# Attention units ordered by block of queries, with plain fp32 P V in column tiles and the projection and norm moved inside them

## The reference, cut to what matters

```
ln   = layernorm(layernorm(x)) * g_l + b_l;  xn = layernorm(ctx) * g_x + b_x
q    = ln @ Wq.T;  k, v = concat(xn @ Wkv.T, ln @ Wlkv.T)      # 4 heads of 64
P    = softmax(rmsnorm(q) * gq * 64**-0.5 @ (rmsnorm(k) * gk).T, context keys masked)
x2   = x + (P @ v) @ Wo.T + bo
x3   = layernorm(x2);  two best of 8 experts by softmax(x3 @ router.T)
out  = x2 + sum over the two of  weight * ((silu(gate) * up) @ w2)   # gate, up = x3 @ w13
```

## Time and profile before

| | us |
|---|---|
| median of 3 runs | 1198.23 |
| lowest and highest | 1196.29, 1199.64 |
| span of the profiled execution, first to last instruction | 1197.7 |
| PE, DVE busy in it | 1054.0 (88%), 774.5 (65%) |
| ACT, POOL busy in it | 656.9 (55%), 518.0 (43%) |

### The profile page before, as it was taken

One profiled execution on the slowest core, in us unless ns is written; L12 is line 12 of the kernel. 1 busy time (PEld: TensorE's weight loads), 2 busy tenths in 40 slices (PEclk: granted clock), 3 DMA queues, 4 the chain that ended last, 5 costly groups with the idle time before them and its releaser, 6 DMA issues.

```text
span 1197.7 us, 19749 instructions
## 1 busy us (share of the span) xinstructions
PE 1054.0 (88%) x4904; PEld 761.3 (64%) x4905; DVE 774.5 (65%) x1474; ACT 656.9 (55%) x867; POOL 518.0 (43%) x525
## 2 busy tenths in 40 slices
PE   3688689999999999999999999999866268999994
PEld 2455457667666666766666766666555257888884
DVE  4999777766766866766766676686554813444442
ACT  1455446777777777777677677777522012333321
POOL 4012125454544654644645554465410014555553
PEclk9899879999999999999999999999977569999998
DMA  5222402112131111231211211111266777333332
GB/s 162 62 71 71 172 16 69 53 40 70 53 113 58 60 46 53 66 114 45 71 48 48 70 53 49 57 58 47 67 184 209 265 248 199 52 49 52 53 53 26
DMA packets 84392, 100.41 MB, mean 84 GB/s; under 512 B 11035, under 2 KB 78044, under 8 KB 83836
## 3 DMA queue, kind: packets, MB, share of 16 engines
q1 hardware_dynamic: 73694, 89.20, 22.8%
q0 software_dynamic: 7488, 10.23, 5.3%
q10 hardware_dynamic: 3166, 0.46, 0.3%
HBM read 57.60 MB, written 42.26 MB: 83 GB/s over the span
## 4 chain that ended last, share of the span: by engine, by line
PE 70%; DVE 10%; ACT 7%; DMA 5%; issue 5%; SPq 1%; ACTq 1%; DVEq 0%; POOL 0%; POOLq 0%
PE bM L1177 9%; PE bPV L1241 8%; PE bPV L1239 8%; PE bPV L1249 8%; PE bS L1221 7%; PE bS L1222 7%; ACT PT L642 4%; DVE mpart L867 3%; DMA xin<-x 3%; PE bA L1129 2%; PE bG L1340 2%; PE bH L1357 1%; ACT Ph L648 1%; PE bY L1340 1%; PE bY L1342 1%
## 5 line engine op out<-in xcount | busy, mean ns | idle before, releaser
L482 POOL TENSOR_TENSOR Pl<-PT,Ph 128x1024 fp32r<-128x1024 f32 x96 | 230.8, 2404 | 348.5 <-ACT Ph L648 348.5
L867 DVE TENSOR_REDUCE mpart<-bM 128x1 f32<-128x464 f32 x524 | 310.9, 635 | 87.2 <-PE bM L1177 85.9
L642 ACT ACTIVATE PT<-bS 128x1024 f32<-128x1024 f32 (+1 forms) x240 | 239.4, 998 | 139.3 <-PE bS L1222 139.3
L648 ACT CAST Ph<-PT 128x1024 fp32r<-128x1024 f32 (+1 forms) x240 | 245.5, 1023 | 7.0
L894 DVE TENSOR_TENSOR Pl<-PT,Ph 128x1024 fp32r<-128x1024 f32 x144 | 176.1, 1223 | 104.6 <-ACT Ph L648 104.4
L1221 PE MATMUL bS<-Q,S 128*128 128x512 f32 x464 | 185.9, 401 | 1.4 <-ACT Q L633 0.7
L1239 PE MATMUL bPV<-Ph,V 128*65 128x512 f32 x464 | 184.5, 398 | 0.0
L1222 PE MATMUL bS<-Q,S 128*128 128x512 f32 x464 | 184.0, 396 | 0.0
L1241 PE MATMUL bPV<-Ph,V 128*64 128x512 f32 x464 | 183.1, 395 | 0.0
L1177 PE MATMUL bM<-S,Q 128*128 128x464 f32 (+1 forms) x524 | 165.5, 390 | 10.9 <-DVE mpart L867 8.7
L1249 PE MATMUL bPV<-Pl,V 128*65 128x512 f32 x464 | 146.9, 395 | 0.8
(11 more groups left out here) (210 smaller groups left out, 1537.4 us busy)
## 6 DMA issues: line engine op xcount, KB each, us to landing
W<-wsp_d SPq DMA_DIRECT2D x32, 768.0 KB, 5.8
wraw<-w SPq DMA_DIRECT2D x96, 128.0 KB, 2.2
wsp_d<-whi SPq DMA_DIRECT2D x96, 128.0 KB, 1.7
wsp_d<-wraw SPq DMA_DIRECT2D x96, 128.0 KB, 1.7
v_d<-Vs SPq DMA_DIRECT2D x29, 258.0 KB, 3.3
V<-v_d SPq DMA_DIRECT2D x4, 1870.5 KB, 7.6
xall<-x SPq DMA_DIRECT2D x1, 2048.0 KB, 13.6
xin<-x SPq DMA_DIRECT2D x16, 128.0 KB, 3.8
```

The source lines that it names most:

```text
L482: pool.tensor_tensor(Pl[:, p % 3, :, :], PT[:, p % 3, :, :], Ph[:, p % 3, :, :].bitcast(F32), ALU.subtract)\
L642: act.activation(PT[:, p % 3, 0:w, :], bS[sl][:, 0:w, :], ACT.Exp).then_inc(sem("exp"), 1)
L648: act.copy(Ph[:, p % 3, 0:w, :], PT[:, p % 3, 0:w, :]).then_inc(sem("p_hi"), 1)
L867: dve.tensor_reduce(mpart[:, i, g:g + 1], banks[k % len(banks)][:, 0:PIECE], AX, ALU.max)\
```

## The change

- Units go by block of queries, then by head: four units in a row make all heads of 512 rows. The loops are written out.
- Queries are kept transposed and scaled in `QT` (two more PE transposes and one ACT copy a row tile in the prologue), so `q_T` and its staging go. The outputs of the heads take their place in `QT`.
- V stays in SBUF, unsplit. P V is plain fp32: for each pair of key tiles two matmuls with 64 columns of weights, which write partitions 0 to 63 and 64 to 127 of bPV. The exponential is used as it is; `Ph` and `Pl` go, and there are four buffers of PT.
- The softmax sums come from adding the PT tiles: 11 additions of 128x1024 a unit on POOL, two on DVE, two merging ones on POOL. `o_T` now has eight plain fp32 matmuls in place of four transposes.
- Projection, residual, norm and logits of 12 row tiles are done in units 4 to 15, one tile a unit; four tiles are left for after the last unit.
- The weight split leaves the attention: experts 4 to 7 are split on POOL in the prologue, in 24 chunks of 512 columns, and DVE waits for all of them before it clears Q2. Experts 0 to 3 are loaded whole when the last exponential is done and are split by ACT and POOL in 12 chunks of 1024 during the routing.

The diff, cut to its core:

```diff
+QW = QB * P
+NPT = 4
+EARLY = 4
-WC = 256
+WC = 512
+SC = 1024
+def run_units(body):
+    for b in range(NB):
+        for h in range(H):
+            body(Unit(b, h))
 # SP
+            for n in range(NSPL):
+                sp.wait_ge(sem("wsplit"), n + 1)
+                sp.dma_start(wsp_d[e, 0, :, c:c + WC], whi[:, n % 2, :].bitcast(F32)).then_inc(sem(f"wst{n % 2}"), 16)
+                sp.dma_start(wsp_d[e, 1, :, c:c + WC], wraw[:, n % 2, :]).then_inc(sem(f"wst{n % 2}"), 16)
+                sp.wait_ge(sem(f"wst{n % 2}"), 32 * (n // 2) + 32)
+                if n + 2 < NSPL:
+                    load(n + 2)
...
+            sp.wait_ge(sem("pv"), NP * UNITS)
+            for i in range(QB):
+                sp.dma_start(x2t[:, i, :], xt[NF + i, :, :]).then_inc(sem(f"xin_t{i}"), 16)
 # POOL
+            run_steps(pool, 0, NC + 2, k_mask)
+            for n in range((E - EARLY) * NCH):
+                pool.tensor_copy(whi[:, n % 2, :], wraw[:, n % 2, :]).then_inc(sem("whi"), 1)
+                pool.tensor_tensor(wraw[:, n % 2, :].bitcast(F32R), wraw[:, n % 2, :],
+                                   whi[:, n % 2, :].bitcast(F32), ALU.subtract).then_inc(sem("wsplit"), 1)
+            def z_sum(w, n):
+                pool.wait_ge(sem("exp"), NP * w.u + max(p, q) + 1)
+                pool.tensor_tensor(acc_p[:], one, PT[:, q % NPT, :, :], ALU.add).then_inc(sem("z_p"), 1)
...
+            for n in range(EARLY * NSC):
+                pool.wait_ge(sem("w_hi"), n + 1)
+                pool.tensor_tensor(W[:, e, 1, c:c + SC], W[:, e, 1, c:c + SC].bitcast(F32),
+                                   W[:, e, 0, c:c + SC].bitcast(F32), ALU.subtract).then_inc(sem("w_in"), 1)
 # ACT
+            def unit(w):
+                    act.activation(PT[:, p % NPT, 0:n, :], bS[(w.h + p) % 2][:, 0:n, :], ACT.Exp).then_inc(sem("exp"), 1)
+                    if p == HEADS_AT and w.h % 2 == 0 and not w.first:
+                        heads_T(w)
+                    if p == SD_AT and w.fin:
+                        sd(w.tile, sd2[:], mv2[:])
+                    if p == X3T_AT and w.fin:
+                        act.copy(x3T[:], bT[:, 0, DIM:2 * DIM].rearrange("p (k c) -> p k c", k=2)).then_inc(sem("x3T"), 1)
+            for e in range(EARLY):
+                act.dma_start(W[:, e, 1, 0:N13]..., w13[e, :, :]...).then_inc(sem(f"raw_e{e}"), 16)
+                act.dma_start(W[:, e, 1, N13:EW]..., w2[e, :, :]...).then_inc(sem(f"raw_e{e}"), 16)
+            o_copy(UNITS)
...
+                act.copy(W[:, e, 0, c:c + SC], W[:, e, 1, c:c + SC].bitcast(F32)).then_inc(sem("w_hi"), 1)
 # DVE
-                    dve.tensor_tensor(Vs[:, t.par, :, D + 1:VW], heads(bV[t.par][:, 0, 0:DIM]),
-                                      Vs[:, t.par, :, 0:D].bitcast(F32), ALU.subtract).then_inc(sem("v_lo"), 1)
+            dve.wait_ge(sem("wsplit"), (E - EARLY) * NCH)
 # PE
-                    for b, c in tiles:
-                        pe.matmul(bPV[0:D + 1, 0, :], V[:, h % 2, c, 0:D + 1], Ph[:, sl, b, :], ...)
-                        pe.matmul(bPV[0:D, 0, :], V[:, h % 2, c, D + 1:VW], Ph[:, sl, b, :], ...)
-                        pe.matmul(bPV[0:D + 1, 0, :], V[:, h % 2, c, 0:D + 1], Pl[:, sl, b, :], ...)
+                    for b, c in enumerate(range(2 * p, min(2 * p + 2, NK))):
+                        last = pe.matmul(bPV[b * D:(b + 1) * D, 0, :], V[:, c, h * D:(h + 1) * D],
+                                         PT[:, p % NPT, b, :], start=c < 2, stop=c >= NK - 2, skip_group_check=True)
+            def o_T(n):
+                for i in range(QB):
+                    pe.matmul(bT[:, 0, at:at + D], oT_a[:, i * P:(i + 1) * P], twin[:], start=True, stop=True)
+                    last = pe.matmul(bT[:, 0, at + D:at + D + 1], acc_d[:, 0, i * P:(i + 1) * P], onec[:], ...)
+                for p in range(NP):
+                    scores(p)
+                    if p == OUT_AT and not w.first:
+                        o_T(u)
+                    if p == HEADS_AT and h % 2 == 0 and not w.first:
+                        heads_T()
+                    if p == Y_AT and w.fin:
+                        project(t, bT[:, 0, 0:DIM])
+                    if p == X3T_AT and w.fin:
+                        x3_T(t, bT[:, 0, DIM:2 * DIM], x3[:])
+                    if p == LG_AT and w.fin:
+                        route(t, bT[:, 0, 0:E], x3T)
+                    pieces(p, 0)
+                    if p >= LAG:
+                        outputs(p - LAG)
+                    pieces(p, 1)
+PIECES = ((0, 1), (2, 0)) + ((2, 1),) * 3 + ((1, 1), (2, 1), (1, 1), (2, 1)) + ((1, 1),) * 5 + ((0, 0),)
+OUT_AT, HEADS_AT, Y_AT, SD_AT, X3T_AT, LG_AT = 5, 7, 8, 9, 11, 12
+LAG = 2
+POOL_SUMS = ((0, 1),) + tuple((-1, p) for p in range(2, 12))
+DVE_SUMS = ((12, 13), (-1, 14))
```

More of the change, by code:

```diff
@@ L312, in load @@
[L312 to L323, removed]
-                sp.wait_ge(sem("wsplit"), NCH * i + ch + 1)
-                for part, buf in enumerate((whi[:, ch % 2, :].bitcast(F32), wraw[:, ch % 2, :])):
-                    half, c = divmod(ch, NCH // 2)
-                    sp.dma_start(wsp_d[4 * e + 2 * part + half, :, c * WC:(c + 1) * WC], buf).then_inc(sem(f"wst{ch % 2}"), 16)
-                sp.wait_ge(sem(f"wst{ch % 2}"), 32 * (NCH // 2 * i + ch // 2) + 64)
@@ L332, in expert_split @@
[L332 to L336, removed]
-            EH = E // H
-            for h in range(H):
-                if h < H - 1:
-                    with sp.Fori(0, EH) as i:
-                        expert_split(EH * h + i, False)
-                else:
-                    for e in range(EH * h, E):
-                        expert_split(e, e == E - 1)
-                if h + 2 < H:
-                    sp.wait_ge(sem("pv"), 3 + NP * NB * (h + 1))
-                    v_load(h + 2)
@@ new lines, in pt_free, with sd @@
+            def pt_free(w, p):
+                old = p - NPT if p >= NPT else max(q for q in range(NP) if q % NPT == p)
+                n = w.u if p >= NPT else w.u - 1
+                act.wait_ge(sem("pv"), NP * n + old + 1)
+                for name, sums in (("z_p", POOL_SUMS), ("z_d", DVE_SUMS)):
+                    for m, pair in enumerate(sums):
+                        if old in pair:
+                            act.wait_ge(sem(name), len(sums) * n + m + 1)
+            def sd(t, to, mv):
+                act.wait_ge(sem("mv2"), t + 1)
+                after(act, sem("rs2"), t)
+                act.activation(to, mv[:, 1:2], ACT.Sqrt, bias=eps[:, 0:1]).then_inc(sem("sd2"), 1)
@@ new lines, in unit @@
+            def unit(w):
+                u, v, t = w.u, w.u + 1, w.tile
+                k = 0
+                for p in range(NP):
+                    if p == OUT_AT and not w.first:
+                        o_out(u, (w.h - 1) % H, w.pairs)
+                    if p == Y_AT and w.fin:
+                        stats2(t, x2[:], bT[:, 0, 0:DIM], st2[:], mv2[:])
+                    if p == SD_AT + 1 and w.fin:
+                        after(dve, sem("ol"), 16 * t)
+                        after(dve, sem("x3T_mm"), t)
+                        norm(t, x2[:], x3[:], mv2[:], sd2[:], rs2[:])
+                    if p == LG_AT + 1 and w.fin:
+                        dve.wait_ge(sem("lg_mm"), t + 1)
+                        dve.tensor_copy(lg[:, t, :], bT[:, 0, 0:E]).then_inc(sem("lg"), 1)
+                    if not w.last:
+                        for _ in range(sum(PIECES[p])):
+                            piece(v, k, M_BANKS)
+                            k += 1
+                        if p == 1:
+                            q_lo(v, w.next_h, w.next_b)
+                if not w.last:
+                    maxima(v)
+                for n in range(ND):
+                    z_sum(w, n)
@@ L917, in _ @@
+            q_lo(0, 0, 0)
             for k in range(NM):
```

829 lines of the change are left out of this document (383 added, 446 removed).

## The result

The changed kernel took 1186.9 us (median of 4 runs, 1183.2 to 1187.4), the kernel before, timed beside it, 1198.9 us: a ratio of 0.9888, 95% interval 0.9868 to 0.9908, so 12 us faster. The forecast was 1180 us and 18 us faster. The profiled execution of the changed kernel spans 1181.3 us, against 1197.7 before.

A forecast was written before the change was run, and what follows sets the result against it. PE was taken to set the pace in attention. From the profiled 1197.7 us, +34 for the split, -3 for attention and -49 for the tail gave 1180 us; range 1125 to 1280.

The forecast's parts named there:

- A2 needs the columns of A1, so it waits; B1 can then start beside A2: P V pair, two records each on lower (A) and upper (B) columns: three record times, 1.29 us a lone pair.
- rival 2: P V: A's matmul runs wholly beside B's, 0.86 us a pair, -120 in place of -10, 1070 us; chance 0.12.
- rival 3: P V: each of 28 width changes a unit costs 0.16 us, 72 us more, 1252 us; chance 0.06.
- -10 for P V: Attention: P V takes 18.5 us a unit against 20.0, less a possible weight-load cost; taken as -10 us in all.
- -16 for waits: Attention: half of the 2.1 us of waits a unit goes, -16 us, with bounds of 0 and -32.
- -7 for the last unit without pieces: Attention: the last unit has no pieces, which saves 6.7 us.
- The small matmuls: Attention: new output transposes, projection and logits on PE add 2.3 us in twelve units; sum +30 us.
- -0.6 a unit: Attention: the gain taken for P V in each unit, -10 us in all.
- The split: Weight split before attention: 24 chunks, 8.3 us per two, end at 173 where Q2 was cleared at 139: +34 us.
- The tail: End of P V to last logits: 21 us (15 to 30) instead of 69.7, -49 us.
- eight issues at 0.35 on ACT's queue: Tail: eight DMA issues at 0.35 us lie beside DVE's and POOL's additions and merges, until 4.5 us after P V.
- Routing keeps its 39: Routing stays at 39 us though ACT and POOL split four experts in it, 12 subtractions at 2.4 = 29 us.

## Why the prediction was right, and where it was not

The sign and the size were right, 12 us against 18. That the sum came so near is luck: the attention came out 28 us better than forecast, the routing 22 worse and the start 7 worse. Two of the five stages were missed, and P V was near in its price by another mechanism.

*P V.* The step "A2 needs the columns of A1, so it waits; B1 can then start beside A2" failed: the two tiles run beside each other whole, as rival 2 had it (four records 1.01 us against 1.86 in the same columns). In the same half no two records start together; in different halves they start two by two, at 501.44 and 501.92, so each two must be one of A and one of B, and B1 does not wait for A2. The step "each change between full and half width empties the array", rival 3, was held against by the 65 and 64 columns that alternate at 0.23 before; it holds all the same between 128 and 64, at 0.34 us by the rows for both changes of a pair, where the rival had said 0.32. Why 65 and 64 columns in fp32r show nothing of it is open. The two nearly cancel: 0.86 + 0.35 = 1.21 a pair, forecast 1.29. Each rival alone would have missed by far (1070 and 1252); the prediction priced them as if only one could hold, and both did. That the pair came within 0.08 us of the forecast is luck. The Trainium skill ("TensorEngine Tiling (Array Packing)", Key Properties) has the drain without a price; the runs put one on it.

*Attention.* By the steps from one start to the next in PE's timeline, P V and the pieces together take 67 us less over the stage, where the forecast had -33: -10 for P V, -16 for waits and -7 for the last unit without pieces. The small matmuls take 36 us more (forecast +30). -67 + 36 = -31, as measured. Two terms were mis-sized. P V costs 13 x 1.21 + 2.1 = 17.8 us a unit, not the 19.4 of "-0.6 a unit", which is 26 us in 16 units. And of the 2.1 us of waits not half but all except some 0.4 go, which is 10 us.

*The split.* Right, with its mechanism and within 7 us. POOL started at 78 and not at 74, since the prologue lost only 1 us with its V subtraction and not 5; a chunk took 4.27 and not 4.15.

*The tail.* Right, -45 against -49. What was priced as lying beside other work, eight issues at 0.35 on ACT's queue, was on the path: one lasted 4.01 us. With four of them in front of the copy the tail took 20.0 us, where the forecast had 21.

*The routing.* The step "Routing keeps its 39" failed. The prediction counted POOL's 28 us of subtractions and asked only who waits for POOL. It did not ask what they do to the instructions of another engine that run at the same time, and that was 22 us.

*The experts.* Forecast 0, measured -3; in the versions that change nothing there the stage takes 226.4 to 230.3 us.

## What to carry to other kernels

Plain fp32 in column tiles is worth it where both tiles are there at once, and every return to full width costs about 0.3 us, so tiles are best issued in groups. A helper engine's long elementwise instructions do not belong beside a chain of short two-input instructions on VectorE: here the chain was held for each one's whole length, and the profile shows it as busy time. When work is moved in front of a stage, ask first where it could start, not how long it takes.

## What the runs showed of the hardware

- Two fp32 matmuls in different halves of the columns run fully side by side, both records of each: 1.01 us for four records of 512 columns, 1.86 in the same half.
- Going from 128 to 64 columns and back in plain fp32 costs 0.34 us by the rows, and the time bears it out (59 us where the rows make 62); going from fp32r to fp32 and back at full width costs nothing that the rows show (0.42 for two pieces, 1.93 for four records and a piece).
- A DVE instruction with two SBUF inputs, or a copy or TENSOR_SCALAR from SBUF, lasts 2.0 to 2.3 us instead of 0.17 to 0.29 while POOL subtracts 1024 columns in SBUF, and 0.36 to 0.77 while it subtracts 256; reductions (0.29), reciprocals (0.25), and a copy from PSUM (0.29), are not held.
- A DMA issue on ACT's queue that usually takes 0.4 to 1.0 us took 4.01 us as the seventh in a row of 0.5 and 1 MB loads (3.8 to 4.5 in the other traces with eight in a row); with four in a row none took over 0.9. What holds it is open.
